# Attention values of two pairs in one product from batch 1 on, and other places for VectorE's rotation and GpSimd's reciprocal roots

## What is computed

```
xn = layernorm(x)
q = xn @ wq.T; lat = xn @ w_kv_down.T; k = lat @ w_k_up.T; v = lat @ w_v_up.T
q, k = rotate(q), rotate(k)                       # cos and sin by position
probs = softmax(q @ k.T / 8 + causal)             # per head
s = (probs @ v) @ wo.T
e_star = max(topk_idx of (xn @ gate_w + gate_b), 2 best)
g = silu(2 * (gelu(xn @ w1[e] + b1[e]) @ w2[e] + b2[e]))   # e = e_star of the token
out = x + s * g
```

## Time and profile before

| | us |
|---|---|
| median of 3 executions | 305.23 |
| lowest, highest | 305.18, 305.68 |
| the profiled execution, its time | 305.23 |
| the profiled execution, its span from first to last instruction | 303.5 |

### The profile page before, as it was taken

How to read it: one execution, slowest core, us unless ns; L and a number is a source line. 1 busy time by engine, 2 the same in 40 slices (tenths; PEclk the granted TensorE clock), 3 DMA queues, 4 the chain that set the end, 5 groups by cost and what they waited for, 6 DMA issues and landing times.

```text
span 303.5 us, 8596 instructions
## 1 busy us (share of the span) xinstructions
PE 290.1 (96%) x2362; PEld 234.8 (77%) x2362; DVE 227.1 (75%) x905; ACT 243.2 (80%) x871; POOL 217.2 (72%) x321
## 2 busy tenths in 40 slices
PE   8897999999999999999999999999999999899994
PEld 3665888888888888777777789999877777676763
DVE  4889998987786998988888524444398899897651
ACT  4387889898977789989898677777779989799982
POOL 3468878687777779999999963333158999899730
PEclk9999999999999999999999999999999999999999
DMA  6854594979433333333334490000513344344200
GB/s 203 251 132 116 104 297 116 236 172 303 101 68 65 67 77 83 101 88 98 89 88 109 96 288 6 2 2 0 154 38 83 100 120 117 93 115 123 61 19 17
DMA packets 39596, 33.35 MB, mean 110 GB/s; under 512 B 4801, under 2 KB 36674, under 8 KB 39554
## 3 DMA queue, kind: packets, MB, share of 16 engines
q1 hardware_dynamic: 38098, 30.51, 39.1%
q0 software_dynamic: 1024, 2.10, 2.5%
q10 hardware_dynamic: 432, 0.23, 0.3%
HBM read 11.07 MB, written 4.98 MB: 53 GB/s over the span
## 4 chain that ended last, share of the span: by engine, by line
PE 66%; POOL 12%; issue 8%; DVE 6%; DMA 3%; ACT 2%; SPq 2%; POOLq 1%; DVEq 0%; ACTq 0%
PE bank L1128 9%; PE bank L1116 9%; PE bank L1142 8%; PE bank L1339 7%; PE bank L1156 6%; PE bank L1327 6%; POOL probs L477 4%; POOL staged L466 4%; PE bank L1090 4%; PE bank L1144 3%; PE bank L1118 3%; DVE masked L602 2%; PE bank L1106 2%; POOL xn L493 2%; DMA z<-in_woT 2%
## 5 line engine op out<-in xcount | busy, mean ns | idle before, releaser
L906 ACT ACTIVATE pexp<-masked,negmax 128x128 f32<-128x128 f32 (+1 forms) x256 | 114.1, 453 | 2.2 <-DVE negmax L602 2.2
L477 POOL TENSOR_SCALAR probs<-pexp,rden 128x256 f32<-128x256 f32 (+1 forms) x184 | 80.3, 451 | 24.3 <-DVE rden L609 21.7
L602 DVE CUSTOM_DVE_ANT_0 masked<-bank,mask 128x128 f32<-128x128 f32 (+1 forms) x256 | 75.9, 352 | 25.2 <-PE bank L1118 25.0
L466 POOL TENSOR_TENSOR staged<-rot_out 128x512 f32<-128x512 f32 x63 | 80.1, 1273 | 17.5 <-DVE rot_out L593 16.9
L593 DVE TENSOR_TENSOR rot_out<-bank,rot 128x1024 f32<-128x1024 f32 x64 | 77.6, 1214 | 3.9 <-PE bank L1092 2.7
L928 ACT COPY probsT<-bank 128x384 f32<-128x384 f32 x128 | 55.0, 481 | 23.8 <-PE bank L1128 22.8
L1128 PE MATMUL bank<-ident,probs 128*128 128x128 f32 x384 | 54.1, 275 | 1.3 <-POOL probs L477 0.6
L906 ACT ACTIVATION_READ_ACCUMULATOR pexp<-masked,negmax 128x1 f32 x256 | 50.0, 195 | 0.0
L1116 PE MATMUL bank<-qk_sb 64*128 64x256 f32 x256 | 45.0, 427 | 3.2 <-DVE negmax L602 2.5
L1128 PEld LDWEIGHTS bank<-ident,probs 128*128 128x128 f32 x384 | 43.1, 140 | 4.1 <-issue 1.5
L1156 PE MATMUL bank<-vo_sb,ctxT 128*128 128x128 f32 x256 | 39.5, 279 | 0.7 <-ACT ctxT L935 0.7
(11 more groups left out here) (114 smaller groups left out, 485.6 us busy)
## 6 DMA issues: line engine op xcount, KB each, us to landing
qk_sb<-staged SPq DMA_DIRECT2D x128, 128.0 KB, 2.7
w_sb<-in_w SPq DMA_DIRECT2D x2, 1024.0 KB, 6.1
w_sb<-in_w SPq DMA_DIRECT2D x4, 512.0 KB, 4.8
sorted_x<-z SPq DMA_DIRECT2D x1, 1408.0 KB, 8.0
sorted_g<-z SPq DMA_DIRECT2D x1, 1152.0 KB, 5.9
out<-res SPq DMA_DIRECT2D x8, 128.0 KB, 1.9
x_sb<-in_x SPq DMA_DIRECT2D x3, 256.0 KB, 3.3
rot<-in_c_rot SPq DMA_DIRECT2D x1, 512.0 KB, 5.8
```

Of the source, the lines that this page charges most:

```text
L466: pool.tensor_tensor(staged[:, n % 2, :, m % 2, :], rot_out[:, m % 2, :, 0:S], rot_out[:, m % 2, :, S:2 * S], op=ALU.add).then_inc(staged_ ...
L477: pool.tensor_scalar(probs[:, g % 2, i, c], pexp[:, g % 2, i, c], rden[:, g % 2, i, k:k + 1], 1.0, ALU.mult, ALU.mult).then_inc(probs_read ...
L602: t = dve.tensor_tensor_reduce(masked[:, g % 2, i, c], s_bank[i][:, c], mask[:, c], -1.0, -NEG * 1e8, ALU.add, ALU.min, negmax[:, g % 2, i ...
L906: e = act.activation(pexp[:, g % 2, i, c], masked[:, g % 2, i, c], ACT.Exp, bias=negmax[:, g % 2, i, k:k + 1], scale=-1.0, accum_out=rowsu ...
```

## The change

Three things change.

1. `FIRST_DOUBLE` goes from 24 to 8. So 16 pairs, 8 to 23, leave `ALONE` and are multiplied two by two in slots 10, 12, ..., 24. Their `output` comes a slot later, and `take_y` (L776) of batches 1 and 2 moves from slots 18 and 26 to 19 and 27.
2. On VectorE `rotate` goes ahead of the extra work of its slot in slots 8 to 16. In slots 1 to 7 and from 17 on it stays last.
3. On GpSimd `rstd` goes behind `rotated` in slots 1, 5 and 9.

```diff
-FIRST_DOUBLE = 3 * NP
+FIRST_DOUBLE = NP
 ALONE = tuple(range(FIRST_DOUBLE)) + (G_LEAD - 2, G_LEAD - 1, B * NP - 2, B * NP - 1)
...
-                if g in (1, 5, 9):
-                    rstd(2 + g // 4)
                 if g == G_LEAD - 1:
                     first_weights()
                 for m in items(g):
                     rotated(m)
+                if g in (1, 5, 9):
+                    rstd(2 + g // 4)
...
                     denominators(g + 1)
                     scale(g + 1)
+                if FIRST_DOUBLE <= g < COUNT_SLOT - 1:
+                    for m in items(g):
+                        rotate(m)
...
                     finalise(FINALS[g])
-                for m in items(g):
-                    rotate(m)
+                if not FIRST_DOUBLE <= g < COUNT_SLOT - 1:
+                    for m in items(g):
+                        rotate(m)
```

## The result

| | before | after |
|---|---|---|
| median of 7 executions each, us | 305.58 | 306.99 |
| lowest, highest | 305.18, 306.29 | 306.23, 307.55 |
| ratio of after to before, 95% interval | | 1.0045 [1.0030, 1.0059] |
| the profiled execution: time, span | 305.23, 303.5 | 306.64, 304.6 |

The kernel became slower by 1.4 us. In the profiled executions it is 1.4 in time and 1.2 in span. Half of that 0.7 is the base: the forecast was worked out from 305.23, and the median of before is 305.58 here.

A forecast was written before the change was run, and what follows sets the result against it. TensorE was taken to bound the kernel from slot 2 to 39, with other engines nearly late at `project`. Savings and new waits summed to +1.12 on 305.23, giving 306.3 us, with an 8-in-10 range of 305.0 to 307.1.

The forecast's parts named there:

- that 0.7: The whole kernel: the forecast of 306.3 us was 0.7 below the measured median of after.
- +0.95: Slot 3: the later root delays `normalise` and the rotation of item 8, so TensorE waits +0.95 us (0.8 to 1.5).
- the 0.4 more of my estimate from it: Slot 2: by the skill's lock rule `normalise` first stands up to 0.4 us longer, making the sum 306.7.
- Rival B: Slots 3 and 7: the later root is hidden, so no 0.95 and 0.10; 305.3 us or no change; chance 0.13.
- Doubling: Slots 9 to 24: eight doubles replace sixteen lone values, saving TensorE 0.16 us each, -1.28 us in all.
- Rival D: Doubled values: two calls of 256 columns stream as long as one of 512, saving nearly nothing; 307.6 us; chance 0.03.
- +0.81 and +0.64: Slots 18 and 20: after shorter odd slots TensorE waits for VectorE's rotation, adding 0.81 and 0.64 us.
- A: Slots 18 and 20: VectorE reaches the rotations in time, 1.45 us of waits fall away, 304.9 us; chance 0.12.
- the extras that now come behind the rotation lie in VectorE's idle time: Slots 10 to 16: extras behind the rotation fit ahead of the next scores; slot 10's wait goes, -0.10 us.
- Rival C: Slots 9, 11, 13, 15: reciprocals waiting for exponentials make rotations 0.2 late each, +0.8 us, 307.1 us; chance 0.12.
- +0.25: Slot 24: TensorE's transposes come earlier and wait for GpSimd's last part, +0.25 us (0 to 0.6).
- TensorE reaches slot 28 as late as before, and the transfer is there: Slot 28: the wait of 0.25 us for the transfer behind GpSimd's sum goes, -0.25 us.

The follow-up runs named there:

- E1: The changed kernel with the reciprocal roots of slots 1 and 5 back ahead of GpSimd's sums, slot 9's still behind; 306.09 us, ratio to before 1.0004.
- E2: The kernel before with only the reciprocal roots moved behind the sums in slots 1, 5 and 9; 307.03 us, ratio to before 1.0033.
- E11: The kernel before with only VectorE's rotation ahead of the extra work in slots 8 to 16; 305.99 us, ratio to before 1.0000.
- E3: The kernel before with only the values of pairs 8 to 23 doubled, neither of the two moves; 307.52 us, ratio to before 1.0044.
- E4: The changed kernel with the rotation ahead of the extra work up to slot 19 instead of 16; 306.93 us, ratio to before 1.0028.
- The first two groups of experiments: The first eight of twelve follow-up kernels, in two groups of four with the kernel before beside each; before's medians there were 306.03 and 305.73 us.
- the third: The group of the last four follow-up kernels, with the kernel before beside them on the same chip; before's median there was 305.77 us.
- E9: The changed kernel with all three roots (slots 1, 5 and 9) back ahead of GpSimd's sums; 307.47 us, ratio to before 1.0046.
- E8: The changed kernel with the rotation ahead in slots 0 to 16 and without the added doubling, roots behind; 304.92 us, ratio to before 0.9961.

## Why the prediction was right, and where it was not

**Slots 1 to 3 and 5 to 7.** Right in mechanism and size: +0.97 for +0.95. VectorE's `normalise` took 0.84 beside `scale(3)`, where the working had 0.85. That the two agree is partly luck: I had doubled the 0.42 of one half, and the halves took 0.39 and the rest, each until 0.08 behind the end of a part of `scale` (0.37 and 0.48). The Trainium skill ("SBUF — State Buffer", section "SBUF: two separate sides") has an engine hold the port pair for a whole instruction, and the trace agrees with that. But a half that was held up did not then take its full 0.34 besides, so the 0.4 more of my estimate from it did not come. E1 and E2 show the cause from both sides. Rival B is out.

**Doubling.** -0.80 and +0.64 in each of eight pairs of slots is -1.28. In slots 16 and 17 a lone `values` takes 0.80 and a double one 1.44, so the 0.16 is saved in the `values` themselves. Rival D is out: the saving is 0.02 for each matrix product fewer, eight times what it took for one.

**Slots 18 and 20.** The waits are 1.03 and 0.55, the steps +0.90 and +0.63 for +0.81 and +0.64. The 0.09 more in slot 18 goes with the rotation ahead in slot 16 and not with the doubling: `row_max` of slot 17 starts 1.07 behind the slot's begin instead of 0.97, E11 has it too (+0.11), and E3 hasn't (+0.80). Why it starts later isn't shown. E4 shows that they hang on the place of the rotation: with it ahead both go. But they come back as waits for `hot`, `row_max` and the transfer. So A, which needed VectorE to be early by itself, is out as well.

**Slots 10 to 16.** The step "the extras that now come behind the rotation lie in VectorE's idle time" failed in one slot. The extras of slot 9 came under GpSimd's sum, and the chain of roots behind them came into slot 12: +0.41. Rival C had the place (a reciprocal that waits for exponentials) but not the cause, and it was one slot of its four.

**Slots 24 to 28.** +0.28 for +0.25 in slot 24. The step "TensorE reaches slot 28 as late as before, and the transfer is there" failed: the wait stayed at 0.30. GpSimd's sum for it, the one of slot 25, ended 1.13 later than in before (125.68 for 124.55), and TensorE came 1.60 later, so that the margin grew by 0.47, more than the 0.25 that were wanted. But from the end of the sum to the scores it took 4.09, where it had been 3.57. This slower landing took the gain back, and its cause stays open. Timelines of GpSimd, that sum, first before, then after:

```profile
123.29 1.26 POOL L466 TENSOR_TENSOR staged<-rot_out 128x512 f32<-128x512 f32 x1
```

```profile
124.41 1.27 POOL L466 TENSOR_TENSOR staged<-rot_out 128x512 f32<-128x512 f32 x1
```

The output that was left out in slot 10 and put back in 26 gave 0.26 that I had counted at nothing. (The step of slot 10 is -0.17 = 0.64 for the double, -0.17 for the wait, and so -0.64 for the output and what it drew along; at slot 26 +0.38 came back.) The two cancel.

**From slot 38 on.** 0.39 came back in slot 38, in the stretch of the experts and in slots 50 to 52, where I had nothing. In slot 38 it is the transposes, which took 1.07 instead of 1.21. The first two groups of experiments show these 0.13 to 0.15 in seven of eight traces, doubled or not, and the third in none in full. So it may belong to the execution of before rather than to the change; this stays open.

**The sum.** +1.12 was forecast and +1.11 shown by the traces, so the misses of +0.41, +0.22, +0.09, -0.26 and -0.39 nearly cancel, and that was luck. (The steps are rounded; the spans give 1.09.) Between the medians it is 1.41, and the interval of 0.9 to 1.8 holds both.

**How the parts work together.** Doubling alone is 1.0044, and with the rotation ahead it is still 1.0046 (E9). Only with the root of slot 9 behind does it fall to 1.0004 (E1). So in slot 9 the third part of the change is what lets the second work, while in slot 1, where nothing is doubled and the rotation is last, it costs 1 us.

## What to carry to other kernels

A saving on the bounding engine counts only up to the nearest producer that was just in time, so subtract each handover's margin slot by slot before you add savings up. When an instruction is moved on one engine, ask what will now run beside it on the engine that follows it: here small VectorE steps came under GpSimd's sum and took 2.7 to 4.5 times as long, although the idle time had room for them. Look also at the waits that your change leaves alone: moving the rotation ahead in slot 1 took 0.72 from the wait of slot 2 (E8), while the eight doubles cost more than their 1.28. And an order on a shared queue is judged place by place: with the doubling the root of slot 9 is better behind the sum, while the root of slot 1 is better ahead of it where VectorE's rotation stands behind the root.

## What the runs showed of the hardware

Some of VectorE's short steps from SBUF to SBUF last until GpSimd's sum beside them ends, to within 0.16 us: 0.26 became 1.18 (`negmean`), 0.39 became 1.19 (the cast of `hot`), 0.48 became 1.30 (`rank`) and 0.41 became 1.26 (the cast of `pos`). Their own time does not come on top. The same holds beside the shorter parts of `scale`, which is why a step can look only a little slower there. Steps that read a PSUM bank don't: the rotation takes 1.19 to 1.23 and `row_max` 0.28 and 0.42 beside it or not. The reciprocal of 4 numbers (0.17) and the step that gathers the statistics (L631, 0.17 each) don't either. I hadn't expected that the time of an instruction on 4 numbers a partition can depend so much on its place.
